# Two expert stages: the first tile's products ahead of the second tile's transposes, and the second expert split between the first tile's banks

## The reference

```python
x = x + _L0_xattn_ref(_layernorm(x), ctx, ...)  # 8 experts, the gate reads ctx, top 2
x = x + _L0_ffn_ref(_layernorm(x), ...)         # 8 experts, the gate reads x, top 1, capacity 512
x = x + _L1_xattn_ref(...)                      # attention, 16 heads
x = x + _L1_ffn_ref(...)                        # gated feed-forward, quantised
# in an expert layer, for each expert e that a token chose:
h = relu(x @ W1[e] + b1[e])                     # 256 -> 1024
y = h @ W2[e] + b2[e]                           # 1024 -> 256, weighted by the gate
```

## Time and profile before

| | |
|---|---|
| median of 3 runs | 1555.9 us (1555.59 to 1556.89) |
| profiled execution | 1555.87 us, span 1554.2 us |
| TensorE products busy | 1264.6 us (81%) |
| VectorE busy | 1154.8 us (74%) |
| ScalarE busy | 836.4 us (54%) |
| GpSimd busy | 470.6 us (30%) |
| stage `top2` | tiles from 95.2 to about 528 us |
| stage `top1` | front from 541.6, tiles from 603.3 to about 787 us |

### The profile page before, as it was taken

The page is one execution under the profiler, slowest core; times in us unless marked ns, Lnnn a source line. Parts: engine busy times, 40 slices in busy tenths (PEclk is TensorE's granted clock), DMA queues, the critical chain, the costliest instruction groups (busy, mean ns, idle before and its releaser), DMA issues. The chain is left out here.

```text
span 1554.2 us, 31503 instructions
## 1 busy us (share of the span) xinstructions
PE 1264.6 (81%) x10394; PEld 1028.0 (66%) x10395; DVE 1154.8 (74%) x2027; ACT 836.4 (54%) x1273; POOL 470.6 (30%) x487
## 2 busy tenths in 40 slices
PE   6999999999999573999936899999997599930087
PEld 3468888888889532898825888888886254310076
DVE  3869865655556377996528999999997686999754
ACT  4866633333333151663314667767663667897664
POOL 3234755555553303445222222322323000000000
PEclk9999999999999885999965799999987699975599
DMA  9887633232332284773143010000000001454111
GB/s 320 313 268 218 155 52 54 44 52 45 51 46 37 29 277 127 215 195 54 25 112 101 21 28 24 23 27 25 22 15 6 36 1 61 166 207 146 70 55 55
DMA packets 108486, 146.77 MB, mean 94 GB/s; under 512 B 17072, under 2 KB 84400, under 8 KB 106608
## 3 DMA queue, kind: packets, MB, share of 16 engines
q1 hardware_dynamic: 87280, 116.31, 22.7%
q0 software_dynamic: 21120, 29.30, 11.3%
HBM read 92.35 MB, written 53.23 MB: 94 GB/s over the span
## 5 line engine op out<-in xcount | busy, mean ns | idle before, releaser
L734 ACT ACTIVATE top_x_all<-top_h_ps,top_b1T 128x256 f32<-128x256 f32 x440 | 181.2, 474 | 287.3 <-PE top_h_ps L580 287.3
L578 PE MATMUL top_h_ps<-top_xT_hi,top_w_hi 128*128 128x256 f16 x880 | 240.7, 273 | 1.3 <-DVE top_xT_lo L921 0.8
L579 PE MATMUL top_h_ps<-top_xT_lo,top_w_hi 128*128 128x256 f16 x880 | 240.6, 273 | 0.0
L580 PE MATMUL top_h_ps<-top_xT_hi,top_w_lo 128*128 128x256 f16 x880 | 240.6, 273 | 0.0
L596 PE MATMUL top_y_ps<-top_w_hi,top_x_all 128*128 x880 | 239.9, 273 | 0.5 <-DVE top_x_all L934 0.3
L597 PE MATMUL top_y_ps<-top_w_lo,top_x_all 128*128 x880 | 239.9, 273 | 0.0
L598 PE MATMUL top_y_ps<-top_w_hi,top_x_all 128*128 x880 | 239.9, 273 | 0.0
L932 DVE CAST top_x_all<-top_x_all 128x512 f16<-128x512 f32 x220 | 96.5, 439 | 141.5 <-ACT top_x_all L734 141.4
L934 DVE TENSOR_TENSOR top_x_all<-top_x_all 128x512 f16<-128x512 f32 x220 | 153.1, 696 | 7.6
L387 POOL DMA_INDIRECT x_sum<-top_x_all,top_row_of_slot x54 | 92.5, 1712 | 171.9 <-DVE top_x_all L946 144.6
L1749 PE MATMUL ffn_ps<-ffn_dT_hi,ffn_yT 128*128 128x256 f16 x192 | 53.5, 278 | 107.2 <-DVE ffn_yT L2033 107.2
(11 more groups left out here) (321 smaller groups left out, 3169.3 us busy)
## 6 DMA issues: line engine op xcount, KB each, us to landing
top_staged<-in_L_xattn_W SPq DMA_DIRECT2D x32, 512.0 KB, 6.3
top_staged<-in_L_ffn_w SPq DMA_DIRECT2D x32, 512.0 KB, 6.4
up_raw<-ffn_u_all SPq DMA_DIRECT2D x48, 256.0 KB, 2.0
ffn_yT<-up_raw SPq DMA_DIRECT2D x12, 1024.0 KB, 4.8
kv_rows<-top_w_lo SPq DMA_DIRECT2D x32, 256.0 KB, 4.0
attn_kv_in<-kv_rows SPq DMA_DIRECT2D x32, 256.0 KB, 2.6
top_w_lo<-in_ctx SPq DMA_DIRECT2D x4, 1024.0 KB, 9.7
top_x_all<-in_x SPq DMA_DIRECT2D x4, 1024.0 KB, 12.0
```

The source lines that it names most:

```text
L578: nc.tensor.matmul(out, hi, xT_hi[p][:, c, :], start=(c == 0), stop=False)
L579: nc.tensor.matmul(out, hi, xT_lo[p][:, c, :], start=False, stop=False)
L580: last = nc.tensor.matmul(out, lo, xT_hi[p][:, c, :], start=False, stop=(c == DC - 1))
L734: last = nc.scalar.activation(h32[:, fc * R:(fc + 1) * R], h_ps[:, b, q * R:(q + 1) * R], ACT.Relu, bias=b1T[:, bass.ds(e * FC + fc, 1)], ...
```

## The change

It touches `experts` alone, and so both stages.

- A first transfer brings the first four token groups (of the gate's source, in `top1` of x) under a semaphore of their own, `s_first`; the first group of transposes waits only for it. `gate_transposes` of every later group waits for its quarter.
- TensorE starts after three constants (the identity) in place of ten, and waits for the rest ahead of what uses them.
- In `top2`, VectorE makes the shares of the two choices ahead of both choices' masks (before: between them). The gate weights are stored behind key store 15 (before: 20).
- Expert 1 is loaded ahead of `b2`, in `top2` with one key store between two pieces.
- Tile 0: TensorE makes its `layer1` ahead of the transposes of tile 1. ScalarE splits a piece of expert 1 ahead of each of the four banks and makes tile 1's high half behind them; VectorE does likewise, with tile 1's low half behind its four banks.

```diff
--- before.py
+++ after.py
@@ -246,7 +246,7 @@
-        s_x = [sem(f"x_quarter{q}_loaded") for q in range(4)]; s_small = sem("small_loaded"); s_b2 = sem("b2_loaded"); s_gate_in = [sem(f"gate_quarter{q}_loaded") for q in range(4)]
+        s_x = [sem(f"x_quarter{q}_loaded") for q in range(4)]; s_first = sem("first_rows_loaded"); s_small = sem("small_loaded"); s_b2 = sem("b2_loaded"); s_gate_in = [sem(f"gate_quarter{q}_loaded") for q in range(4)]
         s_staged = [sem(f"staged{c}_loaded") for c in range(CPE)]
@@ -290,13 +290,18 @@
                 g_tiles = gate_source.rearrange("(t p) d -> p t d", p=P)
+                sp.dma_start(gate_all[:, 0:GC, :], g_tiles[:, 0:GC, :]).then_inc(s_first, 16)
                 for q in range(4):
-                    sp.dma_start(gate_all[:, q * n:(q + 1) * n, :], g_tiles[:, q * n:(q + 1) * n, :]).then_inc(s_gate_in[q], 16)
+                    rows_q = slice(q * n + (GC if q == 0 else 0), (q + 1) * n)
+                    sp.dma_start(gate_all[:, rows_q, :], g_tiles[:, rows_q, :]).then_inc(s_gate_in[q], 16)
                     if kv is not None and q == 0:
...
                             sp.dma_start(w_kv[i], w.rearrange("(c p) d -> p c d", p=P)).then_inc(s_kvw["rows"], 16)
+            if gate_source is None:
+                sp.dma_start(x_all[:, 0:GC, :], x_tiles[:, 0:GC, :]).then_inc(s_first, 16)
             for q in range(4):
-                sp.dma_start(x_all[:, q * n:(q + 1) * n, :], x_tiles[:, q * n:(q + 1) * n, :]).then_inc(s_x[q], 16)
+                rows_q = slice(q * n + (GC if q == 0 and gate_source is None else 0), (q + 1) * n)
+                sp.dma_start(x_all[:, rows_q, :], x_tiles[:, rows_q, :]).then_inc(s_x[q], 16)
             if gate_source is not None:
@@ -304,10 +309,10 @@
                     sp.dma_start(x_sum[tokens + k * P:tokens + (k + 1) * P], x_all[:, 0, :]).then_inc(s_begun, 16)
-            def load_expert(e):
+            def load_expert(e, first=0, end=CPE):
                 w1_e = w1[e].rearrange("(c p) f -> p c f", p=P)
                 w2_e = w2[e].rearrange("(c p) d -> p c d", p=P)
-                for c in range(CPE):
+                for c in range(first, end):
                     if not (isinstance(e, int) and e == 0):
@@ -333,15 +338,19 @@
                 sp.dma_start(normed[tokens + k * P:tokens + (k + 1) * P, 0:D], n_all[:, 0, :]).then_inc(s_stored, 16)
-            store_kv(12, 21)
+            store_kv(12, 16)
             sp.wait_ge(s_wts, 1)
...
                 sp.dma_start(normed[tokens + k * P:tokens + (k + 1) * P, D:DW], by_token[:, 0, :]).then_inc(s_wstored, 16)
-            store_kv(21, T)
+            store_kv(16, 25)
+            for c in range(CPE):
+                load_expert(1, c, c + 1)
+                store_kv(25 + c, 26 + c)
+            store_kv(29, T)
             sp.dma_start(b2_all[:].rearrange("p e d -> p (e d)"), broadcast_rows(b2, P, E * D)).then_inc(s_b2, 16)
-            with sp.Fori(1, E) as e:
+            with sp.Fori(2, E) as e:
                 load_expert(e)
@@ -449,17 +458,20 @@
         def _(pe):
-            pe.wait_ge(s_const, 10)
+            pe.wait_ge(s_const, 3)
             pe.wait_ge(s_small, 32 + 16 * (bg is not None))
...
             if gate_source is None:
+                pe.wait_ge(s_const, 10)
                 for c in range(DC):
...
             def gate_transposes(g):
-                if g % 2 == 0:
+                if g == 0:
+                    pe.wait_ge(s_first, 16)
+                else:
                     pe.wait_ge(s_gate_in[g // 2] if gate_source is not None else s_x[g // 2], 16)
@@ -607,7 +620,8 @@
                     e = expert(AHEAD * q + i)
-                    if more or i + 1 < n:
+                    alone = first_tile and i == 0
+                    if not alone and (more or i + 1 < n):
                         transpose_in(q, i + 1)
@@ -615,6 +629,8 @@
                             layer2(m - 1 + p, 1 - p, e_before, fc)
+                    if alone:
+                        transpose_in(q, i + 1)
                     e_before = e
@@ -631,8 +647,8 @@
-        def split_hi(act, e):
-            for c in range(CPE):
+        def split_hi(act, e, first=0, end=CPE):
+            for c in range(first, end):
                 act.wait_ge(s_staged[c], 16 * (e + 1))
@@ -723,9 +739,11 @@
-            def hidden(m, p, i):
+            def hidden(m, p, i, split=None):
                 e = act.value_load(expert_of_tile[0:1, bass.ds(i, 1)], min_val=0, max_val=E - 1)
                 for b in range(4):
+                    if split is not None:
+                        split_hi(act, split, b, b + 1)
                     act.wait_ge(s_h[p], 4 * m + b + 1)
@@ -739,10 +757,14 @@
                 for p in range(2):
-                    if 0 < 2 * m + p < E:
+                    if 1 < 2 * m + p < E:
                         split_hi(act, 2 * m + p)
-                    x_high(m + p, 1 - p)
-                    hidden(m, p, 2 * m + p)
+                    if 2 * m + p == 0:
+                        hidden(0, 0, 0, 1)
+                        x_high(0, 1)
+                    else:
+                        x_high(m + p, 1 - p)
+                        hidden(m, p, 2 * m + p)
             with act.Fori(2 * HEAD, M - 1) as m:
@@ -752,8 +774,8 @@
-        def split_lo(dve, e):
-            for c in range(CPE):
+        def split_lo(dve, e, first=0, end=CPE):
+            for c in range(first, end):
                 dve.wait_ge(s_hi, e * CPE + c + 1)
@@ -773,7 +795,9 @@
                     kv_weights_lo(t // (T // 8) - 1)
-                if t % (T // 4) == 0:
+                if gate_source is None and t == 0:
+                    dve.wait_ge(s_first, 16)
+                elif t % GC == 0:
                     dve.wait_ge(s_x[t // (T // 4)], 16)
@@ -885,9 +909,9 @@
+            if choices == 2:
+                shares_of_two()
             for c in range(choices):
-                if c == 1:
-                    shares_of_two()
                 order(V.tensor_tensor(pick_tile[c], lanes(NS), by_lane(slot_div[c][:], NS), ALU.is_equal))
@@ -921,8 +945,10 @@
-            def hidden_split(m, p):
+            def hidden_split(m, p, split=None):
                 for b in range(4):
+                    if split is not None:
+                        split_lo(dve, split, b, b + 1)
                     dve.wait_ge(s_h32[p], 4 * m + b + 1)
@@ -949,16 +975,18 @@
                     m, p = 2 * q + i // 2, i % 2
-                    if not experts_split and 0 < AHEAD * q + i < E:
+                    if not experts_split and 1 < AHEAD * q + i < E:
                         if kv is not None and AHEAD * q + i == 2:
...
                         split_lo(dve, AHEAD * q + i)
-                    x_low(q, i + 1)
-                    hidden_split(m, p)
                     if isinstance(q, int) and q == 0 and i == 0:
+                        hidden_split(0, 0, 1)
+                        x_low(0, 1)
                         dve.wait_ge(s_b2, 16)
                     else:
+                        x_low(q, i + 1)
+                        hidden_split(m, p)
                         result(m - 1 + p, 1 - p, AHEAD * q + i - 1)
```

## The result

The change makes the kernel slower: 1570.9 us median (1565.65 to 1573.57, five runs) against 1556.9 us (1555.59 to 1558.77, five runs), a ratio of 1.0086 with a 95% interval of 1.0065 to 1.0107. A second comparison of the same two programs gave 1.0070 (1.0043 to 1.0096). The forecast was 1563.8 us with a range to 1566.8: the sign was right, the size was 7 us short.

A forecast was written before the change was run, and what follows sets the result against it. TensorE was taken to bound both expert stages. From 1555.87 us, 5.49 - 2.09 + 0.78 - 0.3 = +3.88, plus 2 x 2.05 for the clock, gave +7.98 and 1563.8 us, range 1558.8 to 1566.8.

The forecast's parts named there:

- VectorE's queue in tile 0: Tile 1's start waits for VectorE's four banks and expert 1's pieces: +5.49 us in top-2, +0.78 in top-1.
- the releaser that was to show it: Sign: tile 1's first product near 108.9 and 619.4, released by VectorE's low half of that tile.
- The front: Earlier start of each stage: 0 in top-2 (bounds 0, +0.3), -0.3 us in top-1 (bounds 0, -2.34).
- the gather: Top-2's gather can start sooner, but TensorE is busy with key products: 0, bounds -0.2 and +0.2 us.
- the loads: Expert 1's pieces issued between the last key stores: 0; +1.14 us in either stage were the first piece late.
- the b2 load: In top-1 it stands behind expert 1's pieces but is wanted only at 618 or later: 0.
- What comes back: Top-2's seven steps after tile 1 recover 2.09 us, expert 1 no longer being split under tile 1; bounds 0, 3.42.
- The clock: TensorE idles before tile 1 and falls to half clock in both stages, 2.05 us each; bounds 0 and twice that.
- shares ahead of the picks: Top-2's shares made ahead of both choices' masks: TensorE's waits cancel, 0; bounds -0.2 and +0.2 us.
- rival 4: Slower still: late first piece in each stage (1566.1 us) or late clock rise in each (1567.9); chance 0.08.
- rival 3: Faster: tile 1's low half not held behind four banks, if VectorE's bank time is under TensorE's; 1550.3 us, chance 0.04.

The follow-up runs named there:

- e8: Kernel after with 17 products of no use filling TensorE's wait before tile 1 in both stages; ratio 1.0055 to the kernel before.
- e4: Kernel after, expert 1's pieces still between tile 0's banks, but tile 1's transposes and halves ahead of tile 0's products; ratio 0.9992 to the kernel before.
- e15: Kernel after with tile 1's transposes and halves in the middle of tile 0, and top-1's expert 1 split ahead of tile 1; ratio 0.9980 to before.
- e3: Kernel after with expert 1 split ahead of tile 1 as before, not in pieces between tile 0's banks; ratio 1.0031 to the kernel before.
- e16: Kernel after with 17 useless products in the wait before tile 1 of both stages and shares between the choices again; ratio 1.0066 to the kernel before.
- e6: Kernel before with only the shares of the two choices put ahead of both choices' masks; ratio 1.0008 to the kernel before.
- e13: Kernel after, but in the top-2 stage tile 0's order and expert 1's split as before; ratio 1.0042 to the kernel before.
- e1: Kernel after with the old order around tile 0 and expert 1 split ahead of tile 1 in both stages; ratio 0.9990 to the kernel before.
- e2: Kernel after with the shares worked out between the two choices' masks again; ratio 1.0071 to the kernel before.
- after again: Kernel after, unchanged, executed and compared a second time; ratio 1.0070 to the kernel before.
- e5: Kernel before with only SyncE's queue reordered, expert 1's pieces loaded between the last key stores; ratio 1.0006 to the kernel before.
- before again: Kernel before, unchanged, run against itself; ratio 0.9993.
- e9: Kernel after with shares and top-2 tile order as before, expert 1's pieces between top-2 tile 0's banks, top-1 halves in mid tile 0; ratio 0.9978 to before.
- e10: Kernel after with shares as before, tile 1's transposes and halves in mid tile 0 in both stages, top-2 pieces around the banks; ratio 0.9957 to before.
- e14: Kernel after, but in the top-1 stage tile 0's order and expert 1's split as before; ratio 1.0060 to the kernel before.

## Why the prediction was wrong

**VectorE's queue in tile 0: right.** The forecast was +5.49 and +0.78, the clean trace (e8) has 5.6 and 0.7, at the place forecast; the releaser that was to show it is not named by the profile. e4 and e15 show that it is the halves behind the banks, and the pieces in front of them, that cost.

**The front, the gather, the loads, the b2 load: right within a microsecond.** The +0.6 at the top-2 front lies over the bound of +0.3, but it is no lasting cost: VectorE began the statistics of the first x quarter, which wait for its landing, at 22.28 there, at 21.89 before, and at 21.73 in the second execution of the kernel after. What the top-1 front gains is not resolved. From TensorE's last product of the top-2 stage to tile 0's transposes it is 75.08 and 75.77 us in the kernel after and 76.04 and 75.51 in the kernel before, and the kernels with the new front have from 74.93 to 78.49.

**What comes back: right in size (1.9 to 3.2 us for 2.09), wrong in reason.** It is not that expert 1's split leaves the steps: e3 has it under tile 1 again and gives back 3.3. What fits is VectorE's floor for tile 8, which takes up a late start of TensorE of up to 3 us.

**The clock: this step failed.** "I therefore take a fall in both stages" at 2.05 each counted the right two: in each stage tile 1 was at half clock in six of the seven traces with its transposes behind tile 0 (all but e8), for 1.6 to 2.6 us in top-2 and 2.2 to 2.8 in top-1. e8, where products fill the idle time but for 1.32 and 0.41 us, shows the cause; in e16, where 2.35 and 3.48 us stay idle behind them, the clock fell. But in the first trace there were two more, 1.7 and 1.3 us, for which the sum had nothing: these 3.0 us are about what the expert stages have over the forecast (2.8). The one in the key products belongs to the step "shares ahead of the picks", priced 0 with bounds of 0.2: the waits do cancel, as e6 shows, but the prediction did not ask what three waits with little between them do to the clock. That in tile 0 was seen only in traces that had it at 73 as well. The second execution of the kernel after has neither and ends the expert stages as late, by 2.4 us of the next term.

**A term that was missing: what is not in any row of before.** ScalarE stood still for 1 to 6 us in tile 0 of one stage or the other in nine of eighteen traces, of both tile orders. The old order keeps this from tile 1 (e13's top-2 stage: ScalarE 2.5 us late, tile 1 on time), because tile 1's low half stands ahead of the banks; but not from tile 8, which came 2.4 us later than in e1 with tile 1 at nearly the same time. In the new order the greater part goes into tile 1's start (1.85 us for 2.0 in e2, 2.4 for 2.4 in after again, 1.9 for 2.9 in e13) and lengthens the idle time of TensorE that the half clock follows. The forecast was built on one execution in which it did not happen.

**The rest of the program.** 3.6 us of the first trace's excess lie behind the expert stages. The kernel before itself differs there by 5.8 us between two executions, and e5, which changes nothing there, shows 3.1. By these numbers it is spread of the executions and no effect of the change; a range built on one span should have held it.

Of the rivals, rival 4 (slower still, 0.08) is the nearest, by other means than the two it named; rival 3's condition, VectorE no slower than TensorE in a tile, never held, and the version in the middle reached its time by taking the halves out of the queue. What stays open is what ScalarE waits for, and how the 11 to 13 timed microseconds divide exactly between queue, clock and ScalarE.

## What to carry to other kernels

When the first tile's work is moved ahead of the second's, ask where the second tile's inputs then stand in the queue of every other engine: moved to the middle of the first tile they gave 0.2 to 0.4%, moved to its end they cost 0.7 to 0.9%. Slack that looks like waste in one trace (a low half that is ready 5 us early) may be what keeps a stall that another execution has from the next tile; look at a second execution of the kernel before pricing its removal. New idle time of TensorE is to be priced with the half clock behind it: the idle 2.3 to 6.9 us before tile 1 were followed by it in twelve cases of twelve, for 1.6 to 2.8 us each. Filling that idle time with products kept the clock up in e8, but no gain in time is shown for it.

## What the runs showed of the hardware

ScalarE, with its input ready, began its first or second bank copy of a stage 1.1 to 5.9 us late in nine of eighteen executions (before again, after again, e2, e3, e9, e10, e13, e14, e16). None of the traces of before, after and e5 to e8 has it, nine of the other twelve, taken at other times, do; so no kernel can be called free of it. In the two where it was longest, 4.5 and 5.9 us (e9 and before again), TensorE too stopped in the middle of tile 0, for 1.9 and 2.9 us, with nothing to wait for. The DMA engines were at 0.94 to 1.04 of their time during the 5.9 us, but the first execution of before had 0.93 to 1.14 there and no stall.

In four of the stalls the trace has one packet of the queue kind "instruction" that ends 0.7 to 0.9 us before ScalarE goes on (in before again at 105.11 for 106.36, in after again from 617.34 to 618.44 for 619.26, and in the top-1 stage of e3 and e13). In e2, e9 and e10 there is none by the stall, and before has such packets at 101.46, 106.78 and 613.25 without one. The Trainium skill (Runtime: NRT & Kernel Launch, Instruction fetch mechanics) calls the refill of an engine's instructions mostly hidden; whether it is what ScalarE waited for is not settled here.
